# One third of a modulation matrix loaded from another engine's queue, fewer products on a constant, and rows turned ahead of a fold, in an attention and mixture-of-experts kernel

## The chip, the cores and the metric

The kernel runs on one core of a Trainium2 chip. The metric is the device time of one execution in microseconds (us), as the median of several runs.

## The reference

One block of an adaptive-layernorm transformer, in float32, for 1024 tokens of width 256. Cut to what matters:

```
mod = (silu(c) @ wmod).reshape(6, 256)            # c is 1x256, wmod is 256x1536
sa, ca, ga, sb, cb, gb = mod                      # ga, gb: |.| at least 0.25, sign kept
h = layernorm(x) * (1 + ca) + sa
n = layernorm(h) * gamma + beta
q, k, v = n @ qkv                                 # qkv is 256x768
x = x + ga * (softmax(causal(q k^T / 16)) v @ o_proj + h)
h = layernorm(x) * (1 + cb) + sb
x = x + gb * (moe(h, top 4 of 32 experts, 64 slots each) + shared_mlp(h))
```

## The kernel before

The 1024 tokens are eight tiles of 128 rows, tile i in `xin[:, i]`. Every engine has its program written out by hand, in order, and waits on semaphores. Only the start matters to the change.

**Loads.** SyncE (its queue is called SPq in the profile, its program is at L373) issues, in this order: `c`; `x` in pieces of two tiles (`x_loaded[0]`, `x_loaded[1]`); the first third of `wmod`, which holds `sa` and `ca` (`wmod_a`, 512 KB, L380); `qkv` (768 KB); the other two thirds of `wmod` (`wmod_b`, 1 MB); the last two pieces of `x`; small vectors; `o_proj` (`wo_sb`); then 4 MB of zeros to the results and the weights of the experts. `wmod_a`, `wmod_b`, `qkv` and `wo_sb` all lie in parts of the expert weight buffers and so bear the name w_sb in the profile.

**ScalarE** (ACT, L525) first loads its function table, then computes exp(-c), from which VectorE (DVE) makes silu(c), repeated over 128 columns (`silu_c`, in h2T). **TensorE** (PE, L1282) meanwhile runs 72 products of a constant with itself (`keep_warm`, L1308), whose result nobody reads. Then `mod_rows(0)` (L1295, w_sb and h2T, 128x512) multiplies `silu_c` with `wmod_a`, which puts rows `sa` and `ca`, repeated on all partitions, into bank 0.

**VectorE** takes the moments of the first four tiles of x (`moments(0)`, L806 and L811; the first two tiles need x_loaded[0], the next two x_loaded[1]), gets 1/sqrt from a seed of ScalarE (L546, L547) and a refinement (L827 to L829), and normalizes tiles 1 and 3 (L843), ScalarE tiles 0 and 2 (L554). `make_h(0, 4)` (L853, L857) then multiplies with 1+ca and adds sa out of bank 0. A second norm follows the same way, with ScalarE's `hn_tile` (L570) and VectorE's (L879) writing `rows`.

**TensorE after `mod_rows(0)`**: twelve transposes of `qkv` (L1323), `fold_qk` (Wq Wk^T), `mod_rows(1)`, then, before the change, `fold_vo(0)`, `turn_h(0)`, `turn_h(1)`, `fold_vo(1)`, `project_q(0)`. `fold_vo(k)` is one half of Wv o_proj (L1295, bank with w_sb and arena, two products of 128x256, which the profile shows as x4; it waits for `wo_loaded`). `turn_h(j)` transposes two tiles of the normed rows (L1373, four transposes); it waits for `hn_act` and `hn_dve`. `xn1_evac` (L888) on VectorE reads what `turn_h(1)` made, and `project_q(0)` (L1295, score_pair with arena and w_sb, 128x512) waits for it (`hn1_done`). The values (`project_v`), scores and softmax of the tiles come after that, `scores(i)` at L1419 to L1423, `row_max(i)` on VectorE at L929. The mixture of experts makes up the second half of the span.

Of the kernel before, what the change touches and what calls it, by code (L numbers as in the profile page):

```python
# [39 lines left out]
def adaln_attention_moe(nc, x, qkv, o_proj, gamma, beta, gate_w, gate_bias, w1, w2, w3,  # L40
                        shared_gate, shared_up, shared_down, c, wmod, out):
    _, N, H = x.shape
    E, _, F = w1.shape
    FS = shared_gate.shape[1]
    KT = H // P
# [21 lines left out]
    with ExitStack() as ctx:  # L67
# [40 lines left out]
        wmod_a = place3[:, 0:1024].rearrange("p (k n) -> p k n", k=KT)  # L108
# [101 lines left out]
        wmod_loaded = [sem("wmod_loaded0"), sem("wmod_loaded1")]  # L210
# [140 lines left out]
        MOMENTS = (mv1, mv2, mv3)  # L351

        XHAT_DVE = (1, 3)
        WARM = 72
        VO_BANK = [bank[b] for b in (6, 7, 7, 7)]
        pos_bank = lambda b: bank[(0, 3, 7)[b]]
        POS, SLOTS = 128, (256, 256 + 2 * PAIRS)
# [15 lines left out]
        def _(sp):  # L373

            sp.dma_start(cc[:, 0, :], c.rearrange("a (p k) -> p (a k)", k=KT)).then_inc(c_loaded, 16)
            wmod_d = wmod.rearrange("(p k) n -> p k n", k=KT)
            for j in range(NB):
                sp.dma_start(xin[:, 2 * j:2 * j + 2, :], x_d[:, 2 * j:2 * j + 2, :]).then_inc(x_loaded[j], 16)
                if j == 1:
                    sp.dma_start(wmod_a, wmod_d[:, :, 0:512]).then_inc(wmod_loaded[0], 16)  # L380
                    sp.dma_start(qkv_sb, qkv.rearrange("(p k) n -> p k n", k=KT)).then_inc(qkv_loaded, 16)
                    sp.dma_start(wmod_b, wmod_d[:, :, 512:1536]).then_inc(wmod_loaded[1], 16)
            sp.dma_start(gb_col[:, 0, :], col(gamma)).then_inc(small_loaded, 16)
# [141 lines left out]
        def _(act):  # L525
            a = nc.scalar

            a.add_instruction(mybir.InstLoadActFuncSet(
                name=nc.get_next_instruction_name(), engine=a.engine, act_func_set_id=EXP_LN_TABLES, ins=[], outs=[]))
            steps = [0]  # L530
# [751 lines left out]
        def _(pe):  # L1282
            t = nc.tensor

            def ring_open(name):

                n = ring[name]
                if n >= 2:
                    pe.wait_ge(ring_drained, n - 1)
                return ring_bank(name)  # L1290

            def product(dst, terms):

                for n, (lhsT, rhs) in enumerate(terms):
                    last = t.matmul(dst, lhsT, rhs, start=(n == 0), stop=(n == len(terms) - 1))  # L1295
                return last


            def mod_rows(b):
                w = wmod_b.rearrange("p k (m n) -> p k m n", n=H)[:, :, 0::3] if b else \  # L1300
                    wmod_a.rearrange("p k (m n) -> p k m n", n=H)
                product(MOD_BANK[b][:, :].rearrange("p (m n) -> p m n", n=H),
                        [(silu_c[:, k, :], w[:, k]) for k in range(KT)]).then_inc(mod_mm, 1)

            def keep_warm(count):

                for _ in range(count):
                    t.matmul(bank[1][:, 0:P], ones_bf[:, :], ones_bf[:, :], start=True, stop=True)  # L1308

            pe.wait_ge(consts, 1)  # L1310
            keep_warm(WARM)
            pe.wait_ge(silu_c_done, 1)
# [20 lines left out]
            def fold_vo(k):  # L1333

                if k == 0:
                    pe.wait_ge(ring_drained, ring["wT2"] + 1)
                    pe.wait_ge(wo_loaded, 16)
                last = product(bank[6][:, H * k:H * k + H], [(wT[:, 2, j, k, :], wo_sb[:, j, :]) for j in range(KT)])
                if k == KT - 1:
                    last.then_inc(wvo_mm, 1)  # L1340
# [26 lines left out]
            def turn_h(j):  # L1367
                pe.wait_ge(hn_act, j + 1)
                pe.wait_ge(hn_dve, j + 1)
                b = bank[1] if j == 1 else ring_open(f"hn{j}")  # L1370
                for i in range(2):
                    for k in range(KT):
                        last = t.transpose(b[:, 256 * k + P * i:256 * k + P * i + P], hn[:, 2 * j + i, P * k:P * k + P],  # L1373
                                           ident[:, :])
                last.then_inc(hn1_mm if j == 1 else ring_filled, 1)

            def project_q(half):
                if half:
                    pe.wait_ge(ring_drained, ring["hn3"] + 1)
                else:  # L1380
                    pe.wait_ge(ring_drained, ring["hn0"] + 1)
                    pe.wait_ge(hn1_done, 1)
                pe.wait_ge(wqk_done, 1)
                if half:
                    pe.wait_ge(qT_act, 1)
                    pe.wait_ge(modc_done, 1)
                for d in range(KT):
                    last = product(bank[1 + 2 * d][:, :], [(wqk[:, k, P * d:P * d + P],
                                                            xnT[:, k, 512 * half:512 * half + 512]) for k in range(KT)])
                last.then_inc(qT_mm, 1)  # L1390
# [112 lines left out]
            fold_qk()  # L1503
            pe.wait_ge(wmod_loaded[1], 16)
            mod_rows(1)
            fold_vo(0)
            turn_h(0)
            turn_h(1)
            fold_vo(1)
            project_q(0)  # L1510
            turn_gate()
# [246 lines left out]
```

## Time and profile before

| what | value |
| --- | --- |
| median of 3 runs | 151.42 us (151.39 to 151.52) |
| span of the one profiled execution | 161.2 us |
| own time of the profiled execution beside its span | not given with the profile |
| TensorE (PE) busy | 145.7 us, 90% of the span |
| VectorE (DVE) busy | 111.7 us, 69% |
| ScalarE (ACT) busy | 65.0 us, 40% |
| mean granted TensorE clock | 0.979 |

The span runs from the first to the last instruction of the profiled execution, which was 9.8 us longer than the median run. Times in the views count from the span's start. Busy times of TensorE are modelled: each matmul of a row of several overlaps the next one, so the step from the start of one row to the start of the next tells more than the busy time. "[idle <- X]" in a timeline row is the idle time of the engine before that row and what ended it.

### The profile page before, as it was taken

To read this page: it belongs to the slowest core of one execution; us is meant where nothing else is said; L and a number is where in the kernel's file an instruction comes from. 1 tells how busy PE (TensorE), PEld (TensorE's weight loads), DVE (VectorE), ACT (ScalarE), POOL (GpSimd) and SP (SyncE) were. 2 spreads that over 40 slices of the span, in tenths; PEclk is the share of its full clock that TensorE was granted. 3 is DMA by queue.
4 is the path that set the end of the run, shared out by engine and by line. 5 is a ranking of instruction groups with operands and counts; after the bars stand their busy time and mean duration, and the time that the engine had idled before them with its cause. 6 is when DMAs were issued, how large, how long until landed. Compare 5 with 4: busy or idle time off the path is not lost.

```text
span 161.2 us, 2747 instructions
## 1 busy us (share of the span) xinstructions
PE 145.7 (90%) x915; PEld 105.2 (65%) x915; DVE 111.7 (69%) x394; ACT 65.0 (40%) x173; POOL 48.5 (30%) x71
## 2 busy tenths in 40 slices
PE   7889799999999999999999999717997989699992
PEld 7846548468566775898787887404564555368881
DVE  2848989898986497798759824107672949559994
ACT  3233680486155428749879411101232323131000
POOL 7400004279520000002000077773176536500000
PEclk9999999999999999999999999995699999999999
DMA  4999999999999997001003034543014011159983
GB/s 114 277 385 387 418 418 375 349 348 348 352 348 350 347 349 242 1 28 51 0 5 109 2 76 117 116 116 94 0 47 105 33 48 45 47 151 343 406 283 134
DMA packets 22080, 31.28 MB, mean 194 GB/s; under 512 B 2065, under 2 KB 18231, under 8 KB 22066
## 3 DMA queue, kind: packets, MB, share of 16 engines
q1 hardware_dynamic: 20642, 27.71, 50.6%
q0 software_dynamic: 1424, 3.39, 7.8%
q8 instruction: 7, 0.11, 0.3%
q14 instruction: 7, 0.06, 0.1%
HBM read 23.65 MB, written 8.13 MB: 197 GB/s over the span
## 4 chain that ended last, share of the span: by engine, by line
PE 51%; DVE 26%; issue 7%; another core or an unknown queue 5%; DMA 4%; ACT 4%; SPq 1%; DVEq 0%
PE bank L1638 8%; PE bank L1445 7%; PE score_pair L1497 5%; PE bank L1660 4%; PE score_pair L1423 4%; PE score_pair L1419 4%; DMA w_sb<-in_L_wmod_dram 4%; PE bank L1497 3%; PE bank L1432 2%; PE score_pair L1445 2%; DVE base L1262 2%; PE score_pair L1651 2%; DVE aT L853 2%; PE score_pair L1295 2%
## 5 line engine op out<-in xcount | busy, mean ns | idle before, releaser
L1638 PE MATMUL bank<-w_sb,arena 128*64 128x256 f32 x128 | 18.3, 408 | 1.3 <-issue 1.2
L500 POOL DMA_INDIRECT arena<-token_rows,gather_idx x16 | 16.1, 1009 | 10.3 <-DVE gather_idx L1046 5.8
L509 POOL DMA_INDIRECT results<-arena,res_idx x11 | 11.0, 999 | 13.3 <-DVE arena L1181 10.9
L1445 PE MATMUL bank<-arena 128*128 128x256 f32 x56 | 13.7, 382 | 0.2 <-ACT arena L602 0.2
L1638 PEld LDWEIGHTS bank<-w_sb,arena 128*64 128x64 f32 x128 | 9.0, 145 | 7.5 <-issue 5.2
L473 POOL TENSOR_TENSOR base<-aT,mod 128x256 f32<-128x256 f32 x8 | 5.8, 726 | 24.3 <-DVE aT L857 20.6
L1445 PEld LDWEIGHTS bank<-arena 128*128 128x128 f32 x56 | 10.1, 190 | 2.3 <-issue 1.3
L593 ACT ACTIVATE prob<-score_pair,nmax 128x128 f32<-128x128 f32 (+7 forms) x8 | 5.9, 742 | 11.6 <-DVE nmax L930 11.5
L1651 PE MATMUL score_pair<-ident,h2T 128*128 128x128 f32 x16 | 3.7, 319 | 7.5 <-DVE base L1063 4.3
L1423 PE MATMUL score_pair<-arena 128*128 128x512 f32 (+3 forms) x24 | 10.1, 504 | 0.0
L1419 PE MATMUL score_pair<-arena 128*128 128x512 f32 (+3 forms) x24 | 9.8, 490 | 0.0
L750 ACT COPY prob<-score_pair 128x256 f32<-128x256 f32 x8 | 3.0, 372 | 16.3 <-PE score_pair L1651 9.9
L1660 PE MATMUL bank<-w_sb,prob 128*64 128x256 f32 x64 | 9.2, 412 | 0.0
L1651 PEld LDWEIGHTS score_pair<-ident,h2T 128*128 128x128 f32 x16 | 1.7, 149 | 10.9 <-issue 7.5
L743 ACT ACTIVATE arena<-score_pair,modc 128x256 f32<-128x256 f32 x8 | 4.5, 565 | 10.3 <-issue 5.0
L1155 DVE TENSOR_SCALAR arena<-score_pair,modc 128x256 f32<-128x256 f32 x8 | 4.3, 542 | 6.2 <-remote 4.4
L488 POOL DMA_INDIRECT first_row<-results,first_idx x1 | 1.2, 1247 | 23.6 <-DVE rows L956 23.6
L1170 DVE TENSOR_TENSOR h2T<-h2T,bank 128x256 f32<-128x256 f32 x8 | 3.3, 418 | 6.7 <-ACT h2T L762 3.7
L629 ACT ACTIVATE h2T<-bank,modc 128x128 f32<-128x128 f32 x16 | 6.3, 449 | 4.0 <-PE bank L1453 3.9
L1295 PE MATMUL score_pair<-arena,w_sb 128*128 128x512 f32 x16 | 7.3, 597 | 0.3 <-issue 0.3
L1295 PE MATMUL bank<-arena 128*128 128x256 f32 x32 | 7.5, 382 | 0.0
L1308 PE MATMUL score_pair<-ones_bf 128*128 128x128 bf16 x72 | 6.5, 278 | 1.1 <-POOL ones_bf L433 1.1
(223 smaller groups left out, 345.4 us busy)
## 6 DMA issues: line engine op xcount, KB each, us to landing
w_sb<-in_L_ffn_w_dram SPq DMA_DIRECT2D x12, 1024.0 KB, 12.5
results<-prob SPq DMA_DIRECT2D x1, 4096.0 KB, 15.8
w_sb<-results SPq DMA_DIRECT2D x6, 512.0 KB, 7.9
token_rows<-rows SPq DMA_DIRECT2D x8, 144.0 KB
xin<-in_L_attn_x_dram SPq DMA_DIRECT2D x4, 256.0 KB, 6.4
w_sb<-in_L_wmod_dram SPq DMA_DIRECT2D x1, 1024.0 KB, 9.5
out_dram<-base SPq DMA_DIRECT2D x8, 128.0 KB, 2.3
w_sb<-in_L_attn_qkv_dram SPq DMA_DIRECT2D x1, 768.0 KB, 7.6
```

Of the source, the lines that this page charges most:

```text
L500: nc.gpsimd.indirect_dma_start(out=slot_in[:, r, :], out_offset=None, in_=rows_d, in_offset=bass.IndirectOffsetOnAxis(ap=gather_idx[:, r:r ...
L509: nc.gpsimd.indirect_dma_start(out=results_d, out_offset=bass.IndirectOffsetOnAxis(ap=res_idx[:, r:r + 1], axis=0), in_=ob[g % 4][:, (r % ...
L629: last = a.activation(h2T[:, k, P * i:P * i + P], ring_bank(f"x{i}")[:, P * k:P * k + P], ACT.Identity, bias=modc[:, 1, k:k + 1], scale=mo ...
L1295: last = t.matmul(dst, lhsT, rhs, start=(n == 0), stop=(n == len(terms) - 1))
L1308: t.matmul(bank[1][:, 0:P], ones_bf[:, :], ones_bf[:, :], start=True, stop=True)
L1419: t.matmul(dst[:, 0:w], qT[:, 0, P * i:P * i + P], xnT[:, 0, 512 * b:512 * b + w], start=True, stop=False)
L1423: last = t.matmul(dst[:, 0:w], qT[:, 1, P * i:P * i + P], xnT[:, 1, 512 * b:512 * b + w], start=False, stop=True)
L1445: last = t.matmul(PV_BANK[i][:, 0:H], probT[:, i % 2, j, :], vo[:, j, :], start=(j == 0), stop=(j == i))
L1497: last = t.matmul(SH_BANK[key][:, 256 * c:256 * c + 256], w[:, k, P * ft:P * ft + P], h2T[:, k, 512 * half + 256 * c:512 * half + 256 * c ...
L1638: last = t.matmul(bank[4 + g % 2][CAP * side:CAP * side + CAP, 2 * F * r:2 * F * r + 2 * F], slotT[:, k, CAP * e:CAP * e + CAP], w13_sb[:, ...
L1651: last = t.transpose(bank[2 + g % 2][:, P * r:P * r + P], hid[:, g % 2, r, :], ident[:, :])
L1660: last = t.matmul(bank[6 + g % 2][CAP * side:CAP * side + CAP, H * r:H * r + H], hidT[:, g % 2, r, CAP * side:CAP * side + CAP], w2_sb[:, ...
```

## The change

Three edits. The load of `wmod_a` is issued by ScalarE, as the first instruction of its program, and no longer by SyncE. `keep_warm` runs 56 products, not 72. `turn_h(0)` and `turn_h(1)` stand ahead of `fold_vo(0)`.

```
-        WARM = 72
+        WARM = 56
...
                 if j == 1:
-                    sp.dma_start(wmod_a, wmod_d[:, :, 0:512]).then_inc(wmod_loaded[0], 16)
                     sp.dma_start(qkv_sb, qkv.rearrange("(p k) n -> p k n", k=KT)).then_inc(qkv_loaded, 16)
                     sp.dma_start(wmod_b, wmod_d[:, :, 512:1536]).then_inc(wmod_loaded[1], 16)
...
             a = nc.scalar
 
+            act.dma_start(wmod_a, wmod.rearrange("(p k) n -> p k n", k=KT)[:, :, 0:512]).then_inc(wmod_loaded[0], 16)
             a.add_instruction(mybir.InstLoadActFuncSet(
...
             mod_rows(1)
-            fold_vo(0)
             turn_h(0)
             turn_h(1)
+            fold_vo(0)
             fold_vo(1)
             project_q(0)
```

TensorE's program around `mod_rows(1)`, the piece of the difference with what each row waits for ("w_sb,h2T" is `mod_rows`, "w_sb,arena" `fold_vo`, "ident,rows" `turn_h`, "arena,w_sb" `project_q`):

```order
 L1295 MATMUL score_pair<-w_sb,h2T 128x512 [waits wmod_loaded1]
 L1295 MATMUL score_pair<-w_sb,h2T 128x512
-L1295 MATMUL bank<-w_sb,arena 128x256 [waits wo_loaded,ring_drained]
-L1295 MATMUL bank<-w_sb,arena 128x256
 L1373 MATMUL bank<-ident,rows 128x128 [waits ring_drained,hn_dve,hn_act]
 L1373 MATMUL bank<-ident,rows 128x128 x3
 L1373 MATMUL score_pair<-ident,rows 128x128 [waits hn_dve,hn_act]
 L1373 MATMUL score_pair<-ident,rows 128x128 x3
-L1295 MATMUL bank<-w_sb,arena 128x256 x2
+L1295 MATMUL bank<-w_sb,arena 128x256 [waits wo_loaded,ring_drained]
+L1295 MATMUL bank<-w_sb,arena 128x256 x3
 L1295 MATMUL score_pair<-arena,w_sb 128x512 [waits wqk_done,hn1_done,ring_drained]
```

The two products of `fold_vo(0)` moved from ahead of the eight transposes to behind them, together with the wait for `o_proj`, and stand now in one row with those of `fold_vo(1)`. Ahead of them the only difference is the count of the products on the constant.

ScalarE's program from its start, as it is now (the load is new, everything else is as before):

```order
L523 UNCONDITIONAL_BRANCH [waits barrier_Pool_Activation_PE_DVE_SP_release]
L527 DMA w_sb<-in_L_wmod_dram 128x2x512
L528 ACT_TABLE_LOAD
L550 ACTIVATE cc<-cc 128x2 [waits c_loaded]
L546 ACTIVATE lnv<-mv,eps 128x4 [waits var_done,consts]
```

The load stands ahead of the table load and of the first wait. On SyncE the loads of qkv, of the rest of `wmod` and everything behind them each move up by one place; VectorE's program is the same.

## Rows read from the trace of the kernel before

**Rows 1.** Stretches: PE, PEld, DVE, ACT, POOL busy (count); clock, DMA share, GB/s.

```profile
0.00:2.00 2.00, 0.95 (x10) 0.95 (x11) 0.00 (x0) 1.21 (x1) 1.33 (x11) 1.00 0.02 0
2.00:4.00 2.00, 2.00 (x21) 2.00 (x20) 0.85 (x5) 0.28 (x2) 1.79 (x11) 1.00 0.79 224
4.00:6.00 2.00, 2.00 (x22) 2.00 (x20) 1.88 (x9) 0.00 (x0) 1.84 (x3) 1.00 1.02 252
6.00:8.00 2.00, 1.59 (x28) 1.42 (x25) 1.40 (x7) 1.10 (x4) 0.00 (x0) 1.00 0.94 304
```

**Rows 2.** The chain of waits at the start: start us, us, what.

```profile
2.22 6.02 DMA w_sb<-in_L_wmod_dram
...
8.38 1.97 PE score_pair L1295 x4
```

**Rows 3.** DMA issues of SyncE: x, x, wmod_a, qkv; KB, us to landing.

```profile
xin<-in_L_attn_x_dram SPq DMA_DIRECT2D x1, 256.0 KB, 2.7
...
xin<-in_L_attn_x_dram SPq DMA_DIRECT2D x1, 256.0 KB, 3.0
...
w_sb<-in_L_wmod_dram SPq DMA_DIRECT2D x1, 512.0 KB, 6.0
...
w_sb<-in_L_attn_qkv_dram SPq DMA_DIRECT2D x1, 768.0 KB, 7.6
```

**Rows 4.** Timeline of SyncE's queue: start us, us, what.

```profile
0.80 0.38 SPq L375 DMA_DIRECT2D cc<-in_L_c_dram  x1
1.24 0.94 SPq L378 DMA_DIRECT2D xin<-in_L_attn_x_dram  x2
2.22 0.65 SPq L380 DMA_DIRECT2D w_sb<-in_L_wmod_dram  x1
```

**Rows 5.** Timeline of TensorE, to 28 us.

```profile
1.05 6.54 PE L1308 MATMUL score_pair<-ones_bf 128*128 128x128 bf16 x72 [1.05 <-POOL ones_bf L433]
...
15.91 1.03 PE L1295 MATMUL bank<-w_sb,arena 128*128 128x256 f32 x4
17.42 0.66 PE L1373 MATMUL bank<-ident,rows 128*128 128x128 f32 x4 [0.48 <-ACT rows L570]
18.03 0.66 PE L1373 MATMUL score_pair<-ident,rows 128*128 128x128 f32 x4
18.52 1.03 PE L1295 MATMUL bank<-w_sb,arena 128*128 128x256 f32 x4
19.90 3.67 PE L1295 MATMUL score_pair<-arena,w_sb 128*128 128x512 f32 x8 [0.34 <-issue]
...
27.96 0.60 PE L1419 MATMUL score_pair<-arena 128*128 128x256 f32 x2
```

**Rows 6.** Timeline of ScalarE, its first instruction.

```profile
0.79 1.28 ACT L528 ACT_TABLE_LOAD   x1 [0.79 <-PEq L1746]
```

**Rows 7.** Timeline of VectorE, to 29 us.

```profile
3.97 1.56 DVE L806 BATCH_NORM_STATS2 st<-xin 128x6 f32<-128x256 f32 x4 [0.24 <-DMA xin<-in_L_attn_x_dram]
...
7.41 0.73 DVE L843 TENSOR_SCALAR aT<-xin,rstd,nmr 128x256 f32<-128x256 f32 x2
10.43 1.42 DVE L853 SCALAR_TENSOR_TENSOR aT<-score_pair,aT 128x256 f32<-128x256 f32 x4 [2.29 <-PE score_pair L1295]
...
18.80 1.00 DVE L888 TENSOR_SCALAR arena<-score_pair,gb_col 128x256 f32<-128x256 f32 x2 [0.19 <-PE score_pair L1373]
...
29.14 0.42 DVE L929 TENSOR_REDUCE bmax<-score_pair 128x1 f32<-128x256 f32 x1
```

**Rows 8.** TensorE around its long idle time: timeline row, then stretches with granted clock.

```profile
104.40 1.08 PE L1638 MATMUL bank<-w_sb,arena 128*64 128x256 f32 x8 [1.20 <-issue]
...
105.50:108.00 2.50, 0.00 (x0) 1.00 0.39 105
108.00:109.80 1.80, 0.00 (x0) 0.61 0.44 115
```

**Rows 9.** The page: TensorE's busy share in 40 slices of the span, in tenths.

```profile
PE   7889799999999999999999999717997989699992
```

More of the change, by code:

```diff
@@ L353, in adaln_attention_moe @@
         XHAT_DVE = (1, 3)
-        WARM = 72
+        WARM = 56
         VO_BANK = [bank[b] for b in (6, 7, 7, 7)]
@@ L379, in _ @@
                 if j == 1:
-                    sp.dma_start(wmod_a, wmod_d[:, :, 0:512]).then_inc(wmod_loaded[0], 16)
                     sp.dma_start(qkv_sb, qkv.rearrange("(p k) n -> p k n", k=KT)).then_inc(qkv_loaded, 16)
@@ L526, in _ @@
             a = nc.scalar
+            act.dma_start(wmod_a, wmod.rearrange("(p k) n -> p k n", k=KT)[:, :, 0:512]).then_inc(wmod_loaded[0], 16)
             a.add_instruction(mybir.InstLoadActFuncSet(
@@ L1505, in _ @@
             mod_rows(1)
-            fold_vo(0)
             turn_h(0)
             turn_h(1)
+            fold_vo(0)
             fold_vo(1)
```

## The prediction

> **What bounds the kernel now.** I read the chain of waits first, since an edit at the start is worth only what the chain at the start gives back. The chain runs through the load of `wmod_a`: issued at 2.22, landed at 8.24, then `mod_rows(0)` at 8.38 [rows 2]. VectorE sat idle for 2.29 us before `make_h` could start at 10.43 [rows 7], so TensorE's 72 products, done at 7.59 [rows 5], were not what it waited for. From there the chain is VectorE's and ScalarE's (multiply, add, moments, second norm) up to `turn_h(0)` at 17.42, for which TensorE sat idle 0.48 us [rows 5]. Second, the timeline of TensorE: behind `project_q(0)` at 19.90 [rows 5] it has 9 in nearly every slice until the gathers of the experts at about 100 us [rows 9]. What TensorE gains at `project_q(0)` it can keep, since its program from there is a full queue of work, and what it does not gain there VectorE cannot give it later. Third, SyncE's queue: `c` is issued at 0.80, the two pieces of x from 1.24, `wmod_a` only at 2.22 [rows 4].
>
> **The change part by part.** The sum is made on the profiled execution, whose span (161.2 us) is 9.8 us above the median of the runs (151.42 us); I carry the difference over whole, since all of it arises in the first 20 us. A measurement of this kernel can tell about 0.2% from no change, 0.3 us.
>
> *When the loads land.* ScalarE's first instruction starts at 0.79 [rows 6]; with the load there, `wmod_a` is issued 1.43 us earlier than now. It took 6.0 us from issue to landing behind the pieces of x [rows 3], so by that row it lands at about 6.8. Had it the engines to itself it would be sooner; the lower bound is the 2.7 us of an x piece [rows 3], 3.5, the upper one the landing of now less the head start of 0.44 us (0.79 against 1.24), 7.8.
>
> The pieces of x pay for it. Now the first four moments start at 3.97 as the first piece is there [rows 7], and the second lands at 1.72 + 3.0 = 4.72 (its issue is the second of the pair that starts at 1.24; [rows 3, 4]), just in time for the third moment. The DMA engines are 0.79 busy between 2 and 4 us and 1.02 between 4 and 6 [rows 1], so there is little idle capacity that a second queue could find. Bytes: x, x and `wmod_a` are 1.05 MB. At 224, 252 and 304 GB/s [rows 1] they have been moved by 2 x 0.224 + 2 x 0.252 = 0.95 MB at 6.0 and the last 0.1 MB at 6.3. Now the first bytes move 0.44 us sooner: 5.9. The idle part of the stretch from 2 to 4 is worth another 0.05 MB, 0.2 us: 5.7. The second x piece landed 0.4 us after its bytes by the same count (0.52 MB at 4.3, landing 4.72). If the shares are even, all three loads end together and x lands at T = 6.1. Bounds: 4.72, as now (x goes first), and 7.8 (x goes last, and `wmod_a`'s slow landing comes with it).
>
> *When `make_h` starts.* Three things must be there. VectorE: after the second piece two moments (0.8 us of the 1.56 for four), then from the end of the moments at 5.53 to the last normalized tile at 7.41 + 0.73 = 8.14 are 2.6 us [rows 7]: T + 3.4 = 9.5. TensorE: from landing to `make_h` are 10.43 - 8.24 = 2.19 us, so 6.8 + 2.2 = 9.0. The products on the constant: 53 of them have run by 6.0 (x10, x21, x22) and 28 instructions then take 1.59 us [rows 1], so 56 end at 6.2, ahead of the load; removing 16 of them gains nothing by itself unless the load lands before 7.45, and then frees TensorE for it. So x decides, at 9.5: VectorE's chain moves forward by g = 10.43 - 9.5 = 0.9 us. The load ahead of the table load delays ScalarE's exp(-c) by some 0.65 us at most (the issue of the same load, [rows 4]), to which VectorE's own wait for x gives more room than that.
>
> *What TensorE makes of g.* `turn_h(0)` waits for the normed rows, and moves with them as long as TensorE is free; with `fold_vo(0)` gone from ahead of it that is from 15.91 [rows 5], so g can count up to 1.5. `turn_h(1)` goes to 18.03 - g. Behind it `fold_vo(1)` now starts 0.49 us later, at 18.52 - g; both folds stand there in the change, four matmuls at (1.03 - 0.38)/3 = 0.22 each, eight of them 1.74. So `project_q(0)` can start at 20.26 - g, where the other thing that it waits for, VectorE's copy (18.80 + 1.00 [rows 7], now 0.1 before it), is through at 19.8 - g. The gain there is 19.90 - (20.26 - g) = g - 0.36 = 0.54 us. Of the reordering this is the price: at g = 0 it would cost 0.36 us. With the old order and g = 0.9, `turn_h(0)` waits for the fold only until 15.91 + 0.87 = 16.8, hence TensorE would come out about even; the move pays TensorE nothing below g = 0.9, it lets VectorE and ScalarE go on 0.3 us sooner.
>
> *What follows.* VectorE's side gains the whole g until `row_max(1)`, which reads what TensorE's `scores(1)` from 27.96 makes, and starts at 29.14 [rows 5, 7]; there VectorE has no slack left, and the smaller of the two gains goes on, TensorE's 0.54. Behind it nothing in this part waits for a fixed time. The loads of `qkv`, `wmod_b` and `o_proj` carry the same bytes ahead of them as now; `qkv` took 7.6 us [rows 3] and is needed two microseconds after `mod_rows(0)` is over, time that TensorE spends idle. Edits at nothing: SyncE's queue moving up by one (its loads wait for the DMA engines, not for the issue) and the products removed.
>
> Sum: 151.42 - 0.54 = 150.9 us.
>
> **A rule against the change.** The rows show engines that are full from 2 us on. The Trainium skill, page "DMA: Bandwidth & Descriptors", section "Issuing engines are not separate DMA queues", says that DMAs from whichever engine run on the same 16 DMA engines and interleave, and that issuing from several only saves the issue time; the same page, section "Queues, rings and completion order", adds that a DMA engine empties a whole packet of descriptors from one ring before it turns to the next. By the first rule alone the two loads share, as in my sum. By the second the load that comes first is served whole: that is the second rival.
>
> **The rivals.**
>
> *Slower: `wmod_a` goes ahead of x.* It is issued 0.44 us before x. If its share of each DMA engine is served before x's, both pieces of x land after it, and the last bytes of all three land where they land now less the head start: T = 7.8. `make_h` starts at 11.2, g = -0.8, and with the 0.36 of the reordering `project_q(0)` is 1.1 us late: 152.6 us. It decides against the change from T = 6.7 on (g - 0.36 below 0) and is measurably slower from T = 7.0. For it: `wmod_a` landed 3.5 us after the second x piece, although by the bytes 0.5 MB should take 2 us, so some DMA engines were slow with it, and x could be caught behind it there. Against: the x pieces alone took 2.7 and 3.0 us, and x has two pieces in its queue for one on the other.
>
> *Much faster: x lands nearly as before.* If x is served about as now, the bound is the other two: products until 6.2, `mod_rows(0)` right behind when the load is there, `make_h` at 8.3 to 9.0, g = 1.4 to 1.5 as far as TensorE can use it (free at 15.91). The gain is 1.1 us: 150.3 us. For it: 0.79 of the engines' time in the decisive stretch, not 1.0. Against: then all bytes of `wmod_a` must fit into the gaps.
>
> *No change that can be told.* x at 6.4 to 7.0, or `wmod_a` as late as 7.8 (`make_h` at 10.0, g = 0.4): within 0.3 us of 151.4. A later place where the gain is lost would come out here too.
>
> *Slower by the clock.* TensorE would now have about 2 us of idle time between `mod_rows(0)` and the landing of `qkv` at 10.5. The profile shows a gap of 1.20 us at full clock, and a gap of 4.3 us in which the granted clock fell to half after some 2.9 us [rows 8]; this one lies between. If it fell, the transposes and `fold_qk` would run at half speed and `turn_h(0)` would wait for TensorE, some 1 us later than forecast: 151.9 us.
>
> **How the numbers follow.** The forecast (x between 5.7 and 6.4) 0.42; x early 0.14; no change 0.22; `wmod_a` ahead of x 0.17; the clock 0.05. Hence faster by over 0.3 us 0.56, within 0.3 us 0.22, slower 0.22. The range reaches from the early x (150.3, with 0.2 us for `qkv` landing sooner: 150.1) to x at 7.5 (g = -0.5, 152.3); beyond them is less than 2 in 10.
>
> **What would show it.** In the trace of the changed kernel: x's second piece lands at 5.7 to 6.4, `wmod_a` at 6 to 7.3; VectorE's moments have a gap between the second and the third; `make_h` starts at about 9.5 and no longer waits for TensorE; `turn_h(0)` at 16.5; `project_q(0)` at 19.4; the clock stays up. It is wrong if the moments end after 7.5, if `make_h` still waits for TensorE, or if `project_q(0)` is early and the end is not.

## The result, and the profile after

The changed kernel is slower: a median of 152.75 us (151.38 to 154.52, 20 runs) against 151.63 us of the kernel before (150.94 to 153.25, 20 runs), ratio 1.0055 with a 95% interval of 1.0029 to 1.008, which is 0.8 us (0.4 to 1.2). The ratios here leave out executions in a slower state that this chip sometimes shows, so that they differ a little from the quotient of the medians. A second comparison of the same two, among the experiments, gave 1.0064 (1.0032 to 1.0095). The forecast was 0.5 us faster.

The profiled span of the changed kernel is 150.9 us with a clock of 1.0. That is no gain against the 161.2 us shown for before: a second profile of the kernel before had a span of 150.1 us, so the first one was an odd execution in its second half (its waits for gathers and the fall of the clock at 108 us are not in the second). At `make_h`, at `project_q(0)` and at 98 us the two profiles of before agree to 0.1 us (0.11, 0.12 and 0.11), and these are the places where the profiles are compared here.

First what the DMA engines do. Stretches of 2 us of the changed kernel, columns as in [rows 1]:

```profile
2.00:4.00 2.00, 2.00 (x21) 2.00 (x20) 0.87 (x4) 0.94 (x2) 1.79 (x11) 1.00 0.80 191
4.00:6.00 2.00, 2.00 (x26) 2.00 (x24) 0.00 (x0) 0.00 (x0) 1.83 (x3) 1.00 1.10 380
6.00:8.00 2.00, 2.00 (x13) 0.95 (x10) 1.46 (x4) 0.00 (x0) 0.00 (x0) 1.00 0.98 407
```

Its DMA issues (both pieces of x, then `wmod_a`, which is now ACTq's; KB, us to landing), which answer to [rows 3]:

```profile
xin<-in_L_attn_x_dram SPq DMA_DIRECT2D x1, 256.0 KB, 5.3
...
xin<-in_L_attn_x_dram SPq DMA_DIRECT2D x1, 256.0 KB, 5.5
...
w_sb<-in_L_wmod_dram ACTq DMA_DIRECT2D x1, 512.0 KB, 5.2
```

`wmod_a` lands at 0.80 + 5.2 = 6.0 us, 2.2 us sooner than before. But x's first piece takes 5.3 us instead of 2.7, its second 5.5 instead of 3.0, so it lands at 7.2 instead of 4.7. The queues' share between 1.5 and 3.5 us shows why (q10 is ScalarE's queue, q1 SyncE's; packets, MB, share of the engines' time):

```profile
q10 hardware_dynamic: 109, 0.22, 54.7%
q1 hardware_dynamic: 144, 0.00, 3.6%
```

SyncE's 144 packets there are the tiny ones of `c`; of x nothing has moved, while in the same stretch before SyncE's queue had moved 0.27 MB. `wmod_a` does not share evenly with x, it is served first: only from 3.5 to 4.5 us do both queues move, 0.25 MB on ScalarE's and 0.08 MB on SyncE's, and by 5.8 us all of `wmod_a` has been moved. Now the engines, VectorE first (answers to [rows 7]), then ScalarE with the issue and the table load behind it ([rows 6]), then TensorE ([rows 5]):

```profile
3.63 0.33 DVE L797 COPY h2T<-cc 128x256 f32<-128x256 f32 x1
6.53 1.46 DVE L806 BATCH_NORM_STATS2 st<-xin 128x6 f32<-128x256 f32 x4 [2.57 <-DMA xin<-in_L_attn_x_dram]
...
9.86 0.73 DVE L843 TENSOR_SCALAR aT<-xin,rstd,nmr 128x256 f32<-128x256 f32 x2
10.62 1.42 DVE L853 SCALAR_TENSOR_TENSOR aT<-score_pair,aT 128x256 f32<-128x256 f32 x4
```

```profile
0.80 0.62 ACTq L527 DMA_DIRECT2D w_sb<-in_L_wmod_dram  x1
1.46 1.28 ACT L528 ACT_TABLE_LOAD   x1 [1.46 <-PEq L1746]
```

```profile
1.05 5.43 PE L1308 MATMUL score_pair<-ones_bf 128*128 128x128 bf16 x56 [1.05 <-POOL ones_bf L432]
6.33 1.94 PE L1295 MATMUL score_pair<-w_sb,h2T 128*128 128x512 f32 x4
9.15 1.09 PE L1323 MATMUL bank<-ident,w_sb 128*128 128x128 f32 x8 [0.89 <-DMA w_sb<-in_L_attn_qkv_dram]
...
17.62 0.66 PE L1373 MATMUL bank<-ident,rows 128*128 128x128 f32 x4 [1.96 <-ACT rows L570]
18.22 0.66 PE L1373 MATMUL score_pair<-ident,rows 128*128 128x128 f32 x4
18.72 1.89 PE L1295 MATMUL bank<-w_sb,arena 128*128 128x256 f32 x8
20.45 3.60 PE L1295 MATMUL score_pair<-arena,w_sb 128*128 128x512 f32 x8
...
28.43 0.60 PE L1419 MATMUL score_pair<-arena 128*128 128x256 f32 x2
```

VectorE sits idle 2.57 us before the first moment, for x, and no longer 2.29 us before `make_h`, for TensorE. `make_h` starts at 10.62, 0.19 us later than before. TensorE starts `mod_rows(0)` at 6.33, 2 us sooner, has nothing to do with what it gained and waits: 0.89 us for qkv, 1.23 us between the transposes of `qkv` for ScalarE, which copies them out (L559) and is now late with its tiles of x, and 1.96 us for the normed rows. `project_q(0)` starts at 20.45, 0.55 us later than the 19.90 of before, and from there the delay stays: `scores(1)` is 0.47 us later at 28 us, and the first transposes of the gathered rows (L1622) start at 98.45 against 97.97 and 97.86 in the two profiles of before.

### The profile page after: what moved, and what is told of

It reads as the page before. It is cut to its first block, busy times and chain, and to the rows that moved or that the text cites. A ratio compares the mean times of both kernels' runs of the same rounds, so it can differ in the third digit from the quotient of the medians.

```text
span 150.9 us, 2715 instructions
## 1 busy us (share of the span) xinstructions
PE 141.6 (94%) x899; PEld 102.6 (68%) x899; DVE 112.5 (75%) x394; ACT 65.0 (43%) x173; POOL 48.6 (32%) x71
## 4 chain that ended last, share of the span: by engine, by line
PE 64%; DVE 13%; DMA 10%; issue 3%; ACT 3%; SPq 3%; POOL 1%; POOLq 0%; DVEq 0%; ACTq 0%
PE bank L1638 8%; PE bank L1445 7%; PE bank L1295 7%; PE score_pair L1497 6%; DMA w_sb<-results 5%; PE score_pair L1423 5%; PE score_pair L1419 5%; PE bank L1497 4%; PE score_pair L1295 4%; DMA xin<-in_L_attn_x_dram 3%; PE bank L1660 3%; PE score_pair L1710 3%; DVE st L806 2%; PE bank L1432 2%; PE score_pair L1622 2%
## 5 line engine op out<-in xcount | busy, mean ns | idle before, releaser
L1638 PE MATMUL bank<-w_sb,arena 128*64 128x256 f32 x128 | 17.0, 387 | 0.0
L1638 PEld LDWEIGHTS bank<-w_sb,arena 128*64 128x64 f32 x128 | 8.4, 136 | 5.2 <-issue 2.1
L1445 PEld LDWEIGHTS bank<-arena 128*128 128x128 f32 x56 | 10.1, 190 | 2.5 <-issue 1.4
L1660 PE MATMUL bank<-w_sb,prob 128*64 128x256 f32 x64 | 8.3, 381 | 0.0
L1295 PE MATMUL bank<-arena 128*128 128x256 f32 x32 | 7.5, 382 | 0.0
L929 DVE TENSOR_REDUCE bmax<-score_pair 128x1 f32<-128x128 f32 (+7 forms) x8 | 6.0, 751 | 1.9 <-PE score_pair L1423 1.9
L1295 PE MATMUL score_pair<-arena,w_sb 128*128 128x512 f32 x16 | 7.2, 592 | 0.0
L546 ACT ACTIVATE lnv<-mv,eps 128x1 f32<-128x1 f32 (+1 forms) x9 | 2.7, 295 | 9.9 <-DVE mv L811 9.6
L1308 PE MATMUL score_pair<-ones_bf 128*128 128x128 bf16 x56 | 5.4, 290 | 1.1 <-POOL ones_bf L432 1.1
L1295 PEld LDWEIGHTS bank<-arena 128*128 128x128 f32 x32 | 5.8, 190 | 0.7
L1295 PE MATMUL score_pair<-shd_sb,aT 128*128 128x256 f32 x24 | 6.3, 392 | 0.0
```

The costliest lines, as they stand in the source:

```text
L929: chain(v.tensor_reduce(bmax[:, i:i + 1], score_pair[i % 2][:, 0:n], AX_X, ALU.max))
L1445: last = t.matmul(PV_BANK[i][:, 0:H], probT[:, i % 2, j, :], vo[:, j, :], start=(j == 0), stop=(j == i))
L1638: last = t.matmul(bank[4 + g % 2][CAP * side:CAP * side + CAP, 2 * F * r:2 * F * r + 2 * F], slotT[:, k, CAP * e:CAP * e + CAP], w13_sb[:, ...
L1660: last = t.matmul(bank[6 + g % 2][CAP * side:CAP * side + CAP, H * r:H * r + H], hidT[:, g % 2, r, CAP * side:CAP * side + CAP], w2_sb[:, ...
```

## The experiments

Theory A: at the start, only when VectorE can begin `make_h` counts (g is how much sooner than 10.43 us that is), and the new order of TensorE costs another 0.36 us. The load from ScalarE's queue puts off x. Theory B: late x does no harm, the new order is the loss. Theory C: something later loses the time. Each short diff is cut to the lines that matter, with `...` for arguments. In runs that add lines to the kernel, the line numbers of the views are one or two higher (L1295 becomes L1296 or L1297, L1622 becomes L1623 or L1624).

### The load alone

```
-sp.dma_start(wmod_a, ...)        # behind x's second piece
+act.dma_start(wmod_a, ...)       # ScalarE's first instruction; 72 products, old order
```

> The load alone moves to ScalarE's queue; 72 products and the old order stay. Theory A (the two queues share the DMA engines, x lands late, and TensorE's new order costs 0.36 us on top): x's pieces land at 6.5 and 7.2 us as in the changed kernel, make_h starts at 10.6, project_q(0) at 20.1, 0.2 us behind the kernel before; time +0.2 us, 0.1 to 0.2%. Theory B (late x is harmless, the new order of TensorE is the whole loss): no difference beyond 0.05 us at project_q(0). Theory C (something later, not the start, makes the loss): project_q(0) as before and the time still 0.5% longer.

Ratio 1.0052 (1.0027 to 1.0077). The moments started at 6.70, `make_h` at 10.77 and `project_q(0)` at 20.24, 0.34 us late, all of it g (10.43 - 10.77):

```profile
6.70 1.43 DVE L806 BATCH_NORM_STATS2 st<-xin 128x6 f32<-128x256 f32 x4 [2.73 <-DMA xin<-in_L_attn_x_dram]
...
10.77 1.42 DVE L853 SCALAR_TENSOR_TENSOR aT<-score_pair,aT 128x256 f32<-128x256 f32 x4
...
20.24 3.67 PE L1295 MATMUL score_pair<-arena,w_sb 128*128 128x512 f32 x8 [0.34 <-issue]
```

B is out as the whole loss: the order was the old one, and the kernel is slower than before clear of the noise. At 98 us (L1622 at 98.30) it is 0.33 to 0.44 us behind, at the low end of the 0.4 to 1.2 us that its ratio says.

### The order alone

```
 mod_rows(1)
-fold_vo(0)
 turn_h(0)
 turn_h(1)
+fold_vo(0)
```

> Only the order changes: turn_h(0) and turn_h(1) ahead of fold_vo(0); load and 72 products as before. Theory A: make_h starts at 10.43 as before, turn_h(0) at 17.4, project_q(0) at 20.26 instead of 19.90; time +0.3 to +0.4 us (0.2%). Theory B: +0.8 us, the whole loss. Theory C: no difference up to 20 us.

The timeline of TensorE shows the price that A put on it. It waits 1.75 us for the rows with no fold to fill the time, then both folds stand between `turn_h(1)` and `project_q(0)`:

```profile
17.41 0.66 PE L1373 MATMUL bank<-ident,rows 128*128 128x128 f32 x4 [1.75 <-ACT rows L570]
...
18.51 1.89 PE L1295 MATMUL bank<-w_sb,arena 128*128 128x256 f32 x8
20.24 3.60 PE L1295 MATMUL score_pair<-arena,w_sb 128*128 128x512 f32 x8
```

20.24 against 19.90 is 0.34 us, and L1622 started at 98.22, 0.25 to 0.36 us late. The ratio, 1.0004 (0.9971 to 1.0037), can't tell this from nothing; it does exclude B's 0.8 us (1.005).

### The load and 56 products, old order

```
-WARM = 72
+WARM = 56                        # with the load from ScalarE
```

> The load from ScalarE's queue and 56 products, old order. Theory A: the products are worth nothing, mod_rows(0) runs from 6.3 but make_h waits for x, so all starts behind 10 us are those of the run with the load alone; +0.2 us. A rival: the idle time of TensorE between mod_rows(0) and the transposes costs its clock; then the granted clock falls below 1.0 before 20 us and the time is over 1 us longer.

1.0037 (0.9992 to 1.0081). In this execution x landed 0.4 us sooner than in the run with the load alone (moments at 6.25), `make_h` started at 10.36 and `project_q(0)` at 19.83. x behind another load is a scattered thing: over the four executions with the whole of `wmod_a` ahead of it the moments started at 6.25, 6.53, 6.70 and 6.89. In this profile the clock stayed at 1.0. The interval of the ratio includes no difference, so that the time neither shows nor excludes the loss.

### The load behind x

```
+act.wait_ge(c_loaded, 16)
+act.dma_start(wmod_a, ...)       # issued at 2.56 us; qkv goes out on SyncE at about 2.2
```

> The load is issued by ScalarE, but only when c has landed (about 2.6 us) and so behind x, instead of at 0.8; 72 products, old order. Theory A: it is the place of the load against x that costs; here x lands near 4 and 4.8 us again, wmod_a at 8.2 to 8.8 (issued 0.4 to 0.6 us later than before), make_h at 10.4 to 11.0; time within 0.4 us of before. If the second queue as such delayed x, whatever is issued first, x would land past 6 us here too.

x landed as before (2.8 and 3.0 us after its issue), so a load that is issued behind x on the other queue does not put it off. It is no test of two queues that move bytes at once, since ScalarE's queue moved nothing before 6.0 us. And the estimate for `wmod_a` was badly off: issued at 2.56 it took 8.8 us. By 6.0 us SyncE's queue had moved x and 0.6 MB of `qkv`, and from then to 11 us both queues moved bytes, ScalarE's 0.52 MB, SyncE's the rest of `qkv` and most of `wmod_b`. The ratio is 1.038 (1.0325 to 1.0435).

```profile
w_sb<-in_L_wmod_dram ACTq DMA_DIRECT2D x1, 512.0 KB, 8.8
...
11.47 3.46 PE L1295 MATMUL score_pair<-w_sb,h2T 128*128 128x512 f32 x4 [4.38 <-DMA w_sb<-in_L_wmod_dram]
...
12.00:14.00 2.00, 2.00 (x4) 0.50 1.06 342
```

TensorE was idle for 4.38 us, and right after it the granted clock was 0.50 (1.2 of 2.4 GHz), so that `mod_rows(0)` took 3.46 us instead of 1.96. `make_h` started at 15.02, `project_q(0)` at 24.49.

### The load in two pieces

```
+act.dma_start(wmod_a[:, :, 0:256], ...)
+act.dma_start(wmod_a[:, :, 256:512], ...)
```

> The run with the load alone from ScalarE's queue, but as two loads (sa's columns, then ca's, 256 KB each), one right behind the other on that queue; 72 products, old order. Theory A1 (a DMA engine serves its share of one load whole before it looks at the other queue): x's first piece now gets in between the halves, lands 1 to 2 us sooner than with one load (6.7), near 5.2, its second piece near 6.7, wmod_a at 6.5. Theory A2 (the engines favour the queue that was filled first, until it is empty): x at 6.5 and 7.2 as with one load. Theory A3 (even sharing, byte by byte): as A2, within 0.3 us.

```profile
xin<-in_L_attn_x_dram SPq DMA_DIRECT2D x1, 256.0 KB, 3.9
...
xin<-in_L_attn_x_dram SPq DMA_DIRECT2D x1, 256.0 KB, 5.4
```

A1, as far as the landings go (the kernel was executed once, so there is no comparison of times). x's first piece landed at 1.24 + 3.9 = 5.1, 1.5 us sooner than behind the whole load, though the bytes ahead and beside it are the same; the second at 7.1. That fits engines that finish their share of one load before they take the other queue's next. The Trainium skill, page "DMA: Bandwidth & Descriptors", section "Queues, rings and completion order", says that an engine drains a whole packet of descriptors from one ring before it turns to the next; with the share of a load on one engine taken as one packet, which the page does not say, the traces of the changed kernel (0.22 MB to 0.00 MB above) and of this run agree. A rival was left untested: that the engines take the loads in the order of their issue, whatever the queue. The issues here were at 0.80 (first half), 1.24 (x), 1.46 (second half) and about 1.7 us (x), so that it foretells the same. The run with the load behind x suits it better: `wmod_a` was issued at 2.56, behind `qkv` at 2.22, and its queue moved nothing until most of `qkv` had been moved. Which of the two rules holds stays open; both put x behind a load that was issued ahead of it.

### Half of the load

```
+act.dma_start(wmod_a[:, :, 0:256], ...)      # ScalarE, first
+sp.dma_start(wmod_a[:, :, 256:512], ...)     # SyncE, in the old place
```

> Half of the third of wmod (the columns of sa, 256 KB) is issued first by ScalarE, the other half by SyncE in its old place; 72 products, old order. Theory A: x lands later in proportion to the bytes that are ahead of it on the DMA engines: 2.6 us later with 512 KB ahead, so 1.1 to 1.5 us later here, near 5.2 and 6.0 us; both halves there by 7.5 to 8.2. If instead the delay comes from there being a second active queue at all, x lands past 6.3 us as with the whole load.

x landed at 5.7 and 6.4, the second half at 7.0, `make_h` started at 9.89, `project_q(0)` at 19.36. The second piece of x is 1.7 us later than before with 256 KB ahead of it and 2.5 with 512 KB. So the delay goes with the bytes ahead, and not with there being a second queue. `mod_rows(0)` started right behind the 72 products, which ended near 8 us in this execution. This kernel, too, was executed once.

### c from ScalarE's queue, and with x's second piece

```
-sp.dma_start(cc[:, 0, :], ...)   # SyncE's first load
+act.dma_start(cc[:, 0, :], ...)
```

> All loads on SyncE as before, except that the 1 KB load of c goes to ScalarE's queue, which lets x and wmod_a be issued 0.44 us sooner in the same order. Theory A (what counts is that x and then wmod_a get the DMA engines as early as possible, in this order): x lands at 3.5 and 4.3, wmod_a at 7.8, make_h at 10.0, time 0.4 us shorter (0.3%). Theory that SyncE's issue is not the limit: no difference. If the order of the bytes on the engines does not matter at all, also none.

0.9989 (0.9955 to 1.0022). The loads moved up as expected (`wmod_a` let `mod_rows(0)` start at 7.43), but `make_h` only started at 9.80, held up by VectorE. Its timeline and GpSimd's:

```profile
4.05 1.81 DVE L797 COPY h2T<-cc 128x256 f32<-128x256 f32 x1
5.78 1.39 DVE L806 BATCH_NORM_STATS2 st<-xin 128x6 f32<-128x256 f32 x4
...
9.80 1.42 DVE L853 SCALAR_TENSOR_TENSOR aT<-score_pair,aT 128x256 f32<-128x256 f32 x4
```

```profile
3.90 1.81 POOL L462 MEMSET prob<- 128x2048 f32 x1
```

The copy of `silu_c` took 1.81 us and not 0.32, and ended with GpSimd's fill. It was so in two runs above as well, wherever the copy started after the fill had: with the load behind x (4.08, 1.75 us) and with the load in two pieces (4.29, 1.57 us). Where it started ahead of the fill, at 3.41 to 3.64, it took 0.32 to 0.34 us.

```
+act.dma_start(cc[:, 0, :], ...)
+act.dma_start(xin[:, 2:4, :], ...)           # SyncE: x's first piece, wmod_a, qkv, ...
```

> c and the second piece of x from ScalarE's queue; SyncE has the first piece, then wmod_a, then the rest. 72 products, old order. Theory A: two queues fill the DMA engines better than one (1.05 MB were there at 7.2 us in the changed kernel, at 8.2 before), and here x is not behind wmod_a: x at 4 to 5 us, wmod_a at 7.0 to 7.5, make_h at 9.2 to 9.7, time 0.5 to 0.8 us shorter than before. Rival: x's second piece queues behind wmod_a and lands past 6 us, make_h at 10 or later, no gain.

0.9974 (0.9942 to 1.0007). The bytes came no sooner than with c alone on the other queue (`mod_rows(0)` at 7.69), and the copy met the fill again (4.11, 1.75 us): `make_h` at 9.80. Here that cost next to nothing, since `mod_rows(0)` at 7.69 would have let `make_h` start no sooner than 9.74 (before, `make_h` started 2.05 us after `mod_rows(0)`).

### The fill behind the copy

```
+pool.wait_ge(silu_c_done, 1)
 g.memset(prob[:, :, :], 0.0)                 # with c from ScalarE
```

> The run with c from ScalarE's queue, but GpSimd fills the 128x2048 zeros only after silu_c has been made. With c from ScalarE, VectorE's copy of silu_c came 0.6 us later, fell together with GpSimd's fill (3.9 to 5.7 us) and took 1.81 us instead of 0.32, ending when the fill ended. Theory: the two exclude each other; here the copy takes 0.3 us, the moments start at 4.4, end at 5.9, and make_h waits for TensorE alone, near 9.5 instead of 9.8; time 0.7 to 0.9 us shorter than before. Rival: the copy is slow for another reason (DMA traffic at that time) and takes 1 us or more again.

```profile
4.04 0.29 DVE L798 COPY h2T<-cc 128x256 f32<-128x256 f32 x1
4.25 1.40 DVE L807 BATCH_NORM_STATS2 st<-xin 128x6 f32<-128x256 f32 x4
...
9.86 1.42 DVE L854 SCALAR_TENSOR_TENSOR aT<-score_pair,aT 128x256 f32<-128x256 f32 x4 [1.60 <-PE score_pair L1296]
...
4.40 1.80 POOL L463 MEMSET prob<- 128x2048 f32 x1 [0.43 <-DVE h2T L798]
```

The copy took 0.29 us and the moments ran beside the fill unharmed, so the two kinds of instruction are not slow beside GpSimd in the same way. It moved `make_h` nowhere, since `wmod_a` landed 0.4 us later in this execution than in the one before and TensorE was last again: 9.86. 0.9994 (0.9959 to 1.0029): no gain measured. The Trainium skill, page "SBUF — State Buffer", section "SBUF: two separate sides", says that VectorE and GpSimd share one pair of ports as an exclusive lock that is held for a whole instruction, on VectorE's side only by some kinds of instruction; the 1.81 and 0.29 us agree with it, and so do the moments, if they are not of these kinds, which no run here shows.

### Half of the load behind c

```
+act.dma_start(cc[:, 0, :], ...)
+act.dma_start(wmod_a[:, :, 0:256], ...)
 sp: x, x, wmod_a[:, :, 256:512], qkv, ...    # and the fill behind the copy
```

> Candidate for better than both: c, then half of the third of wmod, from ScalarE's queue; x's pieces and the other half from SyncE's; zeros after silu_c; 72 products, old order. By what was seen (x at 5.7 and 6.4 us with half the load ahead; here x is issued 0.44 us sooner and the half 0.44 us later): x near 4.5 and 5.3, halves there by 6.8, make_h near 8.9 to 9.1, project_q(0) near 18.5 to 18.7; time 1.0 to 1.4 us shorter than before. If x's second piece is still caught behind the half: x at 6, make_h at 9.5, 0.8 us shorter.

0.997 (0.9937 to 1.0002). x landed at 4.0 and 4.7 and the second half of the load at 7.2, but `make_h` started only at 9.85, `project_q(0)` at 19.32: `mod_rows(0)`, at 7.82, was behind the 72 products, which ended near 7.9.

> The same with the new order of TensorE (turn_h(0) and turn_h(1) ahead of fold_vo(0)). Theory A: the new order pays only where TensorE would be late for the rows, and here it is idle again before turn_h(0) in the old order, so project_q(0) starts 0.3 to 0.4 us later than in the run beside it, and the time is 0.3 us longer (0.2%). Rival (the forecast's weaker form): with the rows over 1 us sooner the order is even or better.

With the new order `make_h` started at 9.96 and `project_q(0)` at 19.79; g = 0.47, and 20.26 - 0.47 is 19.79. The ratio, 0.9964 (0.9929 to 0.9999), does not tell it from the old order; L1622 stood at 97.84 against 97.42. The half on SyncE's queue, issued at 1.80, landed at 6.1 in this execution, and VectorE was done with its tiles at 8.66. The load and VectorE's tiles were there long before the 72 products were done, which ended near 8 us, and `make_h` waited 1.30 us for TensorE (the load's issue, then TensorE, then VectorE):

```profile
w_sb<-in_L_wmod_dram SPq DMA_DIRECT2D x1, 256.0 KB, 4.3
...
7.93 1.94 PE L1297 MATMUL score_pair<-w_sb,h2T 128*128 128x512 f32 x4
...
9.96 1.42 DVE L855 SCALAR_TENSOR_TENSOR aT<-score_pair,aT 128x256 f32<-128x256 f32 x4 [1.30 <-PE score_pair L1297]
```

TensorE's rows in the old order and then in the new one:

```profile
7.82 1.94 PE L1297 MATMUL score_pair<-w_sb,h2T 128*128 128x512 f32 x4
...
19.32 3.67 PE L1297 MATMUL score_pair<-arena,w_sb 128*128 128x512 f32 x8 [0.34 <-issue]
```

```profile
18.06 1.89 PE L1297 MATMUL bank<-w_sb,arena 128*128 128x256 f32 x8
19.79 3.60 PE L1297 MATMUL score_pair<-arena,w_sb 128*128 128x512 f32 x8
```

> c and half of the third of wmod from ScalarE, zeros after silu_c, old order, and now 56 products. In the run with 72 the products ended near 7.9 us and mod_rows(0) started right behind them, without a wait for the load. If the products hold it up there, mod_rows(0) starts at 6.5 to 7.2 here, when the halves have landed, make_h at 8.8 to 9.3 instead of 9.85, project_q(0) near 18.3 to 18.8, and the time is 0.9 to 1.4 us shorter than before. Rival: the load was there no sooner than the products ended, and nothing changes by more than 0.2 us. Against both: fewer products could let the clock fall, then it is slower.

With 56 products in the run of the old order they ended at 5.81 and `mod_rows(0)` waited 1.88 us for the load, which was there near 7.6: it started at 7.69, `make_h` at 9.74, `project_q(0)` at 19.20. That is 0.1 us against the run with 72, as the rival said, but it does not show that the products are harmless: the load itself landed at 6.1, 7.2 and 7.6 us in the three executions with these loads. With the 6.1 of the run with the new order, 56 products would have let `make_h` start near 8.7 and not 9.96 (estimated from VectorE's end at 8.66; the load and TensorE's 2.2 us give 8.3). How early the load lands on the whole, and so what the 16 products cost, one profile of each does not tell. The ratio is the smallest of all, 0.9948 (0.9916 to 0.9979), 0.8 us shorter than before, and L1622 started at 97.27, 0.6 to 0.7 us ahead. It is faster than the kernel before clear of the noise, and so than the changed one; its interval overlaps those of the three runs before it.

```profile
1.05 4.76 PE L1310 MATMUL score_pair<-ones_bf 128*128 128x128 bf16 x56 [1.05 <-POOL ones_bf L432]
7.69 1.95 PE L1297 MATMUL score_pair<-w_sb,h2T 128*128 128x512 f32 x4 [1.88 <-DMA w_sb<-in_L_wmod_dram]
...
19.20 3.67 PE L1297 MATMUL score_pair<-arena,w_sb 128*128 128x512 f32 x8 [0.34 <-issue]
```

### The kernel before and the changed kernel, again

> The kernel before, unchanged, timed as if it were a change, for two things: what the comparison makes of no difference (both theories: ratio 1.000, within 0.3%), and a second profile of it. The first one had gathers and a clock fall that no run since shows; if the late part was odd only in that execution, the span here is 150 to 151 us with clock 1.0, and the start is the same: wmod_a lands near 8.2, make_h at 10.4, project_q(0) at 19.9.

1.0003 (0.9964 to 1.0041), clock 1.0, span 150.1 us, `make_h` at 10.32, `project_q(0)` at 19.78, L1622 at 97.86.

> The changed kernel, unchanged, for a second profile and a second comparison. If the loss is the start's alone, its profile shows x's first piece at 6.3 to 6.7 us, project_q(0) at 20.2 to 20.6, the first transposes of the gathered rows at 98.2 to 98.6 against 97.9 in both profiles of before, and a ratio of 1.002 to 1.005. If something later adds to it, the ratio is 1.005 or more while that offset is below 0.5 us.

1.0064 (1.0032 to 1.0095), and the start is worse than in the first profile: the moments at 6.89, `make_h` at 11.01, `project_q(0)` at 20.84, L1622 at 98.86. The two profiles of the changed kernel are 0.5 to 0.6 and 0.9 to 1.0 us behind before at 98 us, and the two comparisons say 0.8 and 1.0 us. Neither case of the expectation came out; the offset at 98 us and the time grew together. What the profiles show by 98 us is within the interval of the time, so that nothing later (theory C) is needed, though a few tenths of it are not excluded. And in this execution the clock fell at the start, which the page's clock row and TensorE's timeline and stretches show:

```profile
PEclk9995999999999999999999999999999999999999
```

```profile
9.54 1.09 PE L1323 MATMUL bank<-ident,w_sb 128*128 128x128 f32 x8 [0.97 <-DMA w_sb<-in_L_attn_qkv_dram]
11.85 0.94 PE L1323 MATMUL bank<-ident,w_sb 128*128 128x128 f32 x4 [1.22 <-ACT arena L559]
12.58 3.34 PE L1295 MATMUL score_pair<-arena 128*128 128x256 f32 x8
...
18.00 0.66 PE L1373 MATMUL bank<-ident,rows 128*128 128x128 f32 x4 [0.37 <-ACT rows L570]
...
11.00:12.00 1.00, 0.15 (x1) 1.00 0.93 248
...
13.00:14.00 1.00, 1.00 (x4) 0.50 1.11 412
```

After idle times of 0.97 us for qkv and 1.22 us between the transposes, the granted clock is 0.50 from about 12 to 15.5 us, and `fold_qk` takes 3.34 us instead of 1.98. It cost nothing here only because the rows came late: TensorE still waited 0.37 us for them. It is not rare. Of the 32 timed executions of the changed kernel 15 have a mean clock of 0.987 to 0.989, like this profile (0.989), and of the 12 with the load and 56 products 5 have 0.989; of the 12 with the load alone it is 2. Of the kernel before it is none of 122. Whether it costs time in those executions is not decided: of the changed kernel's, the ones with the lower clock are longer in the mean by 0.5 us in the first comparison and 0.4 in the second, and with 56 products and the old order they are shorter, all within what the scatter allows.

## Why the prediction was wrong

**What held.** The chain and its arithmetic. `make_h` starts 3.4 us after x's second piece or 2.2 us after `wmod_a`, whichever is later (7.2 + 3.4 = 10.6, measured 10.62), unless the products or a slow copy of `silu_c` hold it up. `project_q(0)` starts at 19.90 - g with the old order and at 20.26 - g with the new one:

| kernel | `make_h` | g | order | worked out | measured |
| --- | --- | --- | --- | --- | --- |
| changed | 10.62 | -0.19 | new | 20.45 | 20.45 |
| changed, again | 11.01 | -0.58 | new | 20.84 | 20.84 |
| load alone | 10.77 | -0.34 | old | 20.24 | 20.24 |
| order alone | 10.41 | 0.02 | new | 20.24 | 20.24 |
| load, 56 products | 10.36 | 0.07 | old | 19.83 | 19.83 |
| c from ScalarE | 9.80 | 0.63 | old | 19.27 | 19.27 |
| half behind c | 9.85 | 0.58 | old | 19.32 | 19.32 |
| the same, new order | 9.96 | 0.47 | new | 19.79 | 19.79 |
| the same, 56 products | 9.74 | 0.69 | old | 19.21 | 19.20 |

The six other profiles of the runs, that with `project_q(0)` at 24.49 among them, agree with it to 0.01 us. That the difference made by 20 us is still there at 98 us held too.

**What failed is one term: "If the shares are even, all three loads end together and x lands at T = 6.1".** x's second piece landed at 7.2 us (7.6 in the second profile), so that g was -0.2 (-0.6) and not 0.9. With T = 7.2 the same sum gives g - 0.36 = -0.55 us, which is what `project_q(0)` shows. The term has two parts.

The shares are not even: `wmod_a` goes ahead. But this alone does not make x land later than 6.1, since by the count of bytes the last of the three loads ends at the same time in either order. What it gave was `wmod_a` at 6.0 us, where the sum had 6.8, and `make_h` had no use for it.

The size is wrong, in the step from the bytes to the landing. The bytes were right: the sum had 1.05 MB moved at 5.7 us, and the two queues had moved 1.07 MB at 5.8. From there the sum allowed 0.4 us until x had landed, and it took 1.4 us. By 6.0 us SyncE's queue had moved 0.62 MB, more than the 0.52 MB of x, so that some of the DMA engines were at `qkv` while others still had a part of x to load: a load lands with the last of its engines. The 0.4 us were taken from an x piece with little ahead of it; by the same count `wmod_a`, whose bytes were in at 6.3, landed at 8.24 before the change, 1.9 us later. Why some engines are that far behind was not tried.

This was the rival "`wmod_a` goes ahead of x" (which the paragraph on the rule calls the second), with a chance of 0.17. It named those slow engines, and said x at 7.8 and 1.1 us of loss; measured were x at 7.2 to 7.6 and 0.5 to 1.0 us. Why it was put too low: I counted x's two pieces against one load, as though two queues with more in them got more, when in these runs the load that was issued first went first. And the load that came first was the one with the shorter way to `make_h`.

**The reordering** was priced rightly at 0.36 us, and the price stands in the sum: the forecast of 0.54 us was g less this price. Of the 0.55 us at `project_q(0)` in the first profile it is the larger part, and without it the changed kernel would have been 0.2 to 0.6 us late there. By the table the new order was never ahead, with g up to 0.5; the g of 0.9 from which it was to be even did not come up in any run.

**The products** were put at nothing and are nothing in the changed kernel. Where half of the load is on the other queue, 72 of them end between 6.5 and 8.1 us (all runs with 72), because their pace rises at a different time in each execution (22 of them ran between 4 and 6 us before the change, 39 in the run with the load alone), and can be what `mod_rows(0)` waits for. In one execution it started 1.8 us after its load had landed (7.93 and 6.1), behind the products. In another, 56 products gave only 0.1 us, since the load landed at 7.6 there.

**The clock** as a rival: it fell in one of the two profiles of the changed kernel, after gaps of 0.97 and 1.22 us, where the forecast had thought of one gap of 2 us (`qkv` landed at 9.1 and not at 10.5), and about half of the timed executions show the same mean clock, where the forecast had put 0.05 on it; in the profile its cost was hidden under the late rows. In the profiles of the two other runs with the whole load ahead (alone, and with 56 products) it stayed up, with gaps as long (0.97 and 1.21 us, 0.75 and 1.23 us). What decides between them was not tried.

## What to carry to other kernels

In these runs a load that went to a second queue to be early was early at the cost of what the first queue was about to load; before moving one, ask which of the two has the longer way to the point where they meet, and let that one go first. Cutting the load in two, or moving only part of it, let the other queue in between. A count of bytes tells when they have been moved, not when a load has landed: with others ahead of it or behind it, add the lag that the trace shows for such a load (here 1.4 and 1.9 us). Idle time that an edit opens on an engine is no gain until something with work in it moves up; where it stands before a wait, work that used to fill it (a fold, here) should stay there.

## What was not expected of the hardware

The rate of the first loads scatters. Between 4 and 6 us the engines moved 380, 344, 375 and 397 GB/s in the four profiles with the whole load ahead on the other queue, and 252, 260 and 273 with all loads on SyncE's (the two profiles of before and the run with the order alone). That looks like a gain from the second queue, but the three executions with half of the load behind c, whose loads are the same, moved 283, 394 and 252 GB/s in this stretch, and the second half landed at 7.2, 6.1 and 7.6 us. So a difference of this size between two profiles need not be the change's; whether two queues are faster was not shown. A load's landing can be over 1 us behind the time at which its bytes would be in by the count. A 128x256 copy on VectorE that starts while GpSimd fills 128x2048 words is over only at its end (0.29 to 0.34 us alone; 1.57 to 1.81 us in the four runs where it started beside the fill, ending 0.14 to 0.15 us behind it in each), while the four moments take 1.40 us beside it and 1.39 us right after it.
